# Attention prologue and slots reordered: GpSimd's casts go last, K's spreads and Wo's split are dealt over slots, deviations travel through memory, first V products follow K

## The chip, the cores and the metric

The kernel runs on one core of one Trainium2 chip. The metric is the device time of one execution in microseconds (us). Each kernel is run several times and the median counts; a profiled execution of its own gives the trace.

## What is computed

A decoder layer without masks on 4 x 2048 tokens of width 512: cross attention on a context of 77 keys with 16 heads, then a feed-forward part of inner width 1408 whose activations and weights are rounded to 8 bits.

```python
x = x + xattn(layernorm(x), ctx, ctx, Wq, Wo)
#   Q, K, V = q @ Wq.T, k @ Wq.T, v @ Wq.T          (16 heads of 32)
#   softmax(Q K / sqrt(32)) V, then @ Wo.T
x = x + ffn(layernorm(x), clip_x, clip_down, w_gate, w_up, w_down)
#   xq = round(x / s) * s, one s for the tensor; weights: one s per row
#   h = quant(silu(xq @ Wg) * (xq @ Wu));  h @ Wd
```

## The kernel before, in words

There are three stages, one after the other: `attend` (up to about 650 us of the span), `expand` and `contract`. The change touches `attend` alone.

**Tiles.** The 8192 tokens are 16 blocks of 512. A block is four items (n = 0 to 63 over the whole input). For the projection of queries an item is one group of 128 channels (4 heads) for all 512 tokens of the block; for statistics and the output projection it is one tile of 128 tokens. A batch is 16 items.

**Slots.** `attend` is a software pipeline written out by hand: `for k in SLOTS` from -9 to 72, and every engine runs its own loop over the same k. `at(k, lag)` is item k + lag. TensorE's order in a slot is: scores of item k-2 (`S`, lines 675 and 679), query product of item k+4 (`Q`, line 690, 12 matmuls; the float32 operands are split in a high and a low part, three products each), transposes of the maxima (line 712) when k % 4 is 1 and of the deviations rs (line 703) when it is 3, the products for the maxima of item k+3 (`S`, line 723, called "score matmuls L723" below), output projection of item k-7 (`O`, line 735), sums and values of item k-2 (`DN` line 751, `A` line 754). PSUM banks `A`, `DN`, `O`, `Q` are single, so a transpose into `A` and the values take turns.

**Other engines.** ScalarE makes the high parts (`xT_h`, `qT_h`, `aT_h`), the exponentials and the 8-bit codes of weights (`w_c`, line 509). GpSimd makes the low parts (`aT_l` line 421, `xT_l` line 425, `qT_l` line 429), casts the codes to bf16 (`w_b`, line 413), spreads K over four heads (`kbd`, line 406) and makes Wo's low part (line 432). VectorE does layernorm statistics, maxima (line 593), the scaling of queries by the deviations (`q32`, line 599, which reads `rsb`), the copy of `rsb` out of `A` (line 603), weight maxima and the residual (line 620). SyncE issues every DMA, in order, and waits in between; a wait there holds back all later DMAs.

**Weights.** One of 46 weight steps (22 for gate and up, 24 for down) starts per slot from slot `W_FIRST`: load, one slot later measured and coded, cast in the same slot as coded and at the head of GpSimd's slot, turned by a DMA transpose in slot +2, stored in slot +3.

**Deviations.** After four tiles of statistics rs is a column per tile (128 x 4). The queries need it along the free axis in every partition: TensorE transposes the broadcast columns into `A`, VectorE copies `A` to `rsb`. The wait for that copy sits on TensorE ahead of lines 751 and 754:

```python
if k % 4 == 3 and at(k, 5):
    pe.wait_ge(rsb_rdy, (k + 5) // 4 + 1)
```

A query product of the first item of a block (k % 4 is 0) waits first for all four low parts `xT_l` of its block.

## Time and profile before

| | |
|---|---|
| median of 3 runs | 1185.84 us (1184.47 to 1187.43) |
| profiled execution | 1187.88 us, span 1186.0 us |
| TensorE busy | 1106.8 us of the span |
| VectorE, ScalarE, GpSimd busy | 802.1, 619.7, 401.5 us |
| mean granted TensorE clock | 0.973 of full |

The span is what the trace covers; the time of an execution is some 2 us more. A busy TensorE is one that has matmuls in flight; a gap before a matmul is printed in brackets with the instruction that released it.

### The profile page before, as it was taken

The page shows a single profiled execution, that of the slowest core. Times are in us where ns is not written, and L with a number is a line of the kernel's source. Part 1 is how long each engine was busy: PE and PEld are TensorE (multiplying, and loading weights), DVE is VectorE, ACT ScalarE, POOL GpSimd, SP SyncE. Part 2 cuts the span into 40 slices and gives each one's busy share as a digit, 9 for nine tenths or more (in the row PEclk, how much of TensorE's full clock was granted, in tenths as well). Part 3 has the DMA queues.
Part 4 walks back from the last instruction along what each step waited for, and adds up shares of the span by engine and source line. Part 5 has one row for each costly group of instructions (what it writes and reads, how often), then busy time and mean ns, then how long its engine had stood idle before and what let it go on. Part 6 is the DMA issues. An engine that isn't in the chain of part 4 may idle for free. (4 is left out here: it accounts for less than half of the span.)

```text
span 1186.0 us, 17468 instructions
## 1 busy us (share of the span) xinstructions
PE 1106.8 (93%) x6173; PEld 625.7 (53%) x6202; DVE 802.1 (68%) x1478; ACT 619.7 (52%) x757; POOL 401.5 (34%) x317
## 2 busy tenths in 40 slices
PE   5988999999999999999999969999999999699898
PEld 4645555655666666666665534444444444244333
DVE  5455667677766776766655567787777777566565
ACT  3346555454555555554544436657566664754450
POOL 5454444355353644343321200000000000357578
PEclk8979999999999999999999979999999999799999
DMA  6234556556454545443215626766767512799977
GB/s 238 69 89 110 157 149 160 150 160 152 146 152 143 166 129 164 130 142 104 75 54 161 223 75 230 250 223 234 241 220 253 171 52 89 320 413 418 422 298 261
DMA packets 138736, 219.23 MB, mean 185 GB/s; under 512 B 59040, under 2 KB 67872, under 8 KB 132768
## 3 DMA queue, kind: packets, MB, share of 16 engines
q1 hardware_dynamic: 138656, 218.19, 56.3%
q8 instruction: 46, 0.75, 0.3%
q14 instruction: 34, 0.28, 0.1%
HBM read 133.48 MB, written 72.48 MB: 174 GB/s over the span
## 5 line engine op out<-in xcount | busy, mean ns | idle before, releaser
L1038 POOL TENSOR_TENSOR c_y<-x,c_y 128x512 f32<-128x512 f32 x64 | 112.7, 1794 | 395.2 <-DVE c_y L1072 380.5
L690 PE MATMUL a_Q<-a_xT,wq 128*128 128x512 f32 x768 | 199.8, 410 | 19.0 <-POOL a_xT L425 16.8
L690 PEld LDWEIGHTS a_Q<-a_xT,wq 128*128 128x128 f32 x768 | 144.2, 194 | 73.4 <-issue 22.6
L960 PE MATMUL e_G<-e_cT,gu 128*128 128x512 bf16 x689 | 180.0, 381 | 2.3 <-ACT e_cT L883 1.5
L924 DVE SCALAR_TENSOR_TENSOR h<-e_U,x_gus,e_sg 128x512 f32<-128x512 f32 x176 | 131.8, 749 | 73.2 <-PE e_U L964 47.4
L869 ACT ACTIVATE e_sg<-e_G,x_gus 128x512 f32<-128x512 f32 x176 | 119.0, 685 | 117.6 <-PE e_G L960 117.6
L964 PE MATMUL e_U<-e_cT,gu 128*128 128x512 bf16 x690 | 179.7, 381 | 0.7
L735 PE MATMUL a_O<-a_wo,a_aT 128*128 128x512 f32 x720 | 176.8, 395 | 0.0
L1110 PE MATMUL c_Y<-dn,gu 128*128 128x512 bf16 x704 | 156.8, 386 | 13.5 <-DVE gu L1065 13.5
L501 ACT ACTIVATE a_qT<-a_q 128x512 fp32r<-128x512 f32 x64 | 40.4, 631 | 216.9 <-DVE a_q L599 216.9
L735 PEld LDWEIGHTS a_O<-a_wo,a_aT 128*128 128x128 f32 x720 | 133.4, 189 | 28.0 <-issue 2.5
L472 ACT ACTIVATE a_pr<-a_S 77x2048 f32<-77x2048 f32 x64 | 120.1, 1876 | 37.1 <-PE a_S L679 37.1
L593 DVE TENSOR_REDUCE a_mx<-a_S 128x16 f32<-128x1232 f32 x64 | 92.1, 1439 | 57.4 <-PE a_S L723 57.4
L560 DVE TENSOR_TENSOR a_att<-a_A,a_lnd 128x512 f32<-128x512 f32 x64 | 44.2, 691 | 118.9 <-POOL a_aT L421 61.1
L1110 PEld LDWEIGHTS c_Y<-dn,gu 128*128 128x128 bf16 x704 | 69.4, 99 | 100.6 <-issue 21.0
L421 POOL TENSOR_TENSOR a_aT<-a_att,a_aT 128x512 fp32r<-128x512 f32 x64 | 82.3, 1285 | 113.7 <-ACT a_aT L475 113.7
L1056 ACT ACTIVATE c_c<-h,h_inv 128x3072 int8<-128x3072 f32 (+1 forms) x32 | 82.5, 2633 | 64.9 <-DVE gu L1065 60.4
L960 PEld LDWEIGHTS e_G<-e_cT,gu 128*128 128x128 bf16 x704 | 69.1, 98 | 85.2 <-issue 1.6
L964 PEld LDWEIGHTS e_U<-e_cT,gu 128*128 128x128 bf16 x704 | 69.1, 98 | 83.9 <-issue 1.4
L928 DVE TENSOR_REDUCE e_hm<-h 128x1 f32<-128x512 f32 x160 | 108.0, 675 | 0.0
L429 POOL TENSOR_TENSOR a_qT<-a_q,a_qT 128x512 fp32r<-128x512 f32 x64 | 82.3, 1285 | 62.4 <-ACT a_qT L501 62.4
L413 POOL CAST w_b<-w_c 128x512 bf16<-128x512 int8 (+1 forms) x34 | 20.3, 597 | 195.9 <-ACT w_c L509 195.9
(128 smaller groups left out, 1351.0 us busy)
## 6 DMA issues: line engine op xcount, KB each, us to landing
x<-x_d SPq DMA_DIRECT2D x32, 1024.0 KB, 7.4
h_d<-h SPq DMA_DIRECT2D x24, 1024.0 KB, 4.1
h<-h_d SPq DMA_DIRECT2D x11, 1536.0 KB, 17.2
a_xr<-in_x SPq DMA_DIRECT2D x64, 256.0 KB, 2.9
a_xt<-in_xT SPq DMA_DIRECT2D x64, 256.0 KB, 3.1
x_d<-a_xr SPq DMA_DIRECT2D x64, 256.0 KB, 2.0
a_xs<-in_x SPq DMA_DIRECT2D x60, 256.0 KB, 2.9
out<-c_y SPq DMA_DIRECT2D x15, 1024.0 KB, 9.7
```

The costliest lines, as they stand in the source:

```text
L472: nc.scalar.activation(pr[:], S[0:KEYS], ACT.Exp, scale=SM_SCALE).then_inc(exped, 1)
L593: nc.vector.tensor_reduce(mx5[:, :, :, n.g], S[:, :, 0:HG * KEYS].rearrange("p t (h k) -> p t h k", h=HG), AX.X, ALU.max).then_inc(maxed, 1)
L690: mm = nc.tensor.matmul(Q[:], wq[:, wp, j, P * n.g:P * (n.g + 1)], xT[:, n.par, xp, j], start=(ins == 0), stop=(ins == 3 * KT - 1))
L735: mm = nc.tensor.matmul(projection(n), aT[:, n.par, ap, j, P * n.g:P * (n.g + 1)], wo[:, wp, j], start=(ins == 0), stop=(ins == 3 * KT - 1))
L869: nc.scalar.activation(sg[:, s], G[:, t % GU], ACT.Silu, scale=gus[:, t:t + 1]).then_inc(silued, 1)
L924: nc.vector.scalar_tensor_tensor(out=h[:, place(u, p), t], in0=U[:, t % GU], scalar=gus[:, IT + t:IT + t + 1], in1=sg[:, s], op0=ALU.mult, ...
L928: nc.vector.tensor_reduce(hm[:, p, t - 1:t], h[:, place(u, p), t - 1], AX.X, ALU.max, apply_absolute_value=True)
L960: mm = nc.tensor.matmul(G[:, t % GU], gu[:, t, k], cT[:, p, k], start=(k == 0), stop=(k == KT - 1))
L964: mm = nc.tensor.matmul(U[:, t % GU], gu[:, IT + t, k], cT[:, p, k], start=(k == 0), stop=(k == KT - 1))
L1038: nc.gpsimd.tensor_tensor(y[:, p, t], x1[:, p, t], y[:, p, t], ALU.add).then_inc(added, 1)
L1056: nc.scalar.activation(c8[:, k % 2, lo:hi], h[:, BUFFER[k], lo:hi], ACT.Copy, scale=hinv[:, 0:1]).then_inc(coded, 1)
L1110: mm = nc.tensor.matmul(Y[:, TT * p + t], cb[:, p, j, P * t:P * (t + 1)], dn[:, :, j], start=(j == 0), stop=(j == IT - 1))
```

## The change

In `attend` six things are rearranged. (1) GpSimd's cast of a code goes to the end of its slot, one slot after the coding; turn and store move one slot back as well. `W_FIRST` goes from 1 to 4. (2) The spread of K for the next batch is one quarter per slot in slots 4 to 7 of a batch, not four at once; Wo's high and low parts are made a quarter per slot (ScalarE from slot -1, GpSimd in slots 0 to 3). (3) From block 1 on, rs goes to memory in four column stores at the end of slot 4b-6 and comes back as a broadcast of 128 x 512 one slot later, both in SyncE's queue; only block 0 uses TensorE's transposes. (4) V's products for batches 0 and 1 follow K's at once, then block 0's transposes; V for batches 2 and 3 come in slots -3 and -2. (5) The query product takes its two products with `xT_h` first and waits for `xT_l` before the third; values, not sums, wait for `A`. (6) Some small VectorE and ScalarE work is dropped (`ve`, the copy of `mv1` to `mom`).

```diff
-W_FIRST = 1
+W_FIRST = 4
@@ sync
+                    if (w := weight(k - W_FIRST - 4)) and w.coded:
+                        store_weight(w)
                     if (w := weight(k - W_FIRST - 3)) and w.coded:
-                        store_weight(w)
-                    if (w := weight(k - W_FIRST - 2)) and w.coded:
                         turn_weight(w)
                     if (w := weight(k - W_FIRST)):
                         load_weight(w)
...
+                    if k % 4 == 2 and (n := at(k, 6)) and n.block > 0:
+                        sp.wait_ge(rs_rdy, n.block + 1)
+                        for t in range(TT):
+                            sp.dma_start(rs_d[n.block, t], rs[:, t:t + 1]).then_inc(rs_out, 16)
+                    if k % 4 == 3 and (n := at(k, 5)) and n.block > 0:
+                        sp.wait_ge(rs_out, 16 * TT * n.block)
+                        sp.wait_ge(q_scaled, n.n)
+                        sp.dma_start(rsb[:], rs_d[n.block].rearrange("t p a -> a (t p)").to_broadcast([P, TOK])).then_inc(rsb_in, 16)
@@ gpsimd
                 for k in SLOTS:
-                    if (w := weight(k - W_FIRST - 1)) and w.coded:
-                        pool.wait_ge(w_coded, w.code + 1)
-                        after(pool, w_turned[w.ring], 16 * (w.code // 2), 1 << 30)
-                        nc.gpsimd.tensor_copy(wb[:, w.ring, 0:w.width], wc[:, w.ring, 0:w.width]).then_inc(w_cast, 1)
-                    if k == -5:
-                        pool.wait_ge(mask_in, 16)
-                        pool.wait_ge(k_hi, GROUPS)
-                        spread_k(0)
...
+                    if 0 <= k < KT:
+                        pool.wait_ge(wo_hi, k + 1)
+                        nc.gpsimd.tensor_tensor(wo[:, 1, k], wo32[:, k], wo[:, 0, k].bitcast(F32), ALU.subtract).then_inc(wo_lo, 1)
+                    b, j = k // PER + 1, k % PER - 4
+                    if 0 <= j < HG and 1 <= b < BATCH:
+                        after(pool, m_scored, PER * (b - 1))
+                        spread_k(b, j)
...
+                    if (w := weight(k - W_FIRST - 2)) and w.coded:
+                        pool.wait_ge(w_coded, w.code + 1)
...
@@ vector
                     if (n := at(k, 4)):
                         dve.wait_ge(q_done, n.n + 1)
                         after(dve, qT_l, n.n)
-                        dve.wait_ge(rsb_rdy, n.block + 1)
+                        if n.block > 0:
+                            dve.wait_ge(rsb_in, 16 * n.block)
                         nc.vector.tensor_tensor(q32[:], Q[:], rsb[:], ALU.mult).then_inc(q_scaled, 1)
-                    if k % 4 == 3 and (n := at(k, 5)):
-                        dve.wait_ge(r_turned, n.block + 1)
-                        after(dve, q_scaled, n.n)
-                        nc.vector.tensor_copy(rsb[:], A[:]).then_inc(rsb_rdy, 1)
@@ tensor
+                project_v(0)
+                project_v(1)
+                pe.wait_ge(rs_rdy, 1)
...
+                for t in range(TT):
+                    mm = nc.tensor.transpose(A[:, P * t:P * (t + 1)], rs[:, t:t + 1].to_broadcast([P, P]), id32[:])
...
-                        pe.wait_ge(xT_l, GROUPS * (n.block + 1))
+                        pe.wait_ge(xT_h, GROUPS * (n.block + 1))
...
-                        for wp, xp in ((0, 0), (0, 1), (1, 0)):
+                        for wp, xp in ((0, 0), (1, 0), (0, 1)):
+                            if xp == 1:
+                                pe.wait_ge(xT_l, GROUPS * (n.block + 1))
...
-                    if k % 4 == 3 and (n := at(k, 5)):
-                        pe.wait_ge(rs_rdy, n.block + 1)
...
-                        if k % 4 == 3 and at(k, 5):
-                            pe.wait_ge(rsb_rdy, (k + 5) // 4 + 1)
```

TensorE at the start of the program, from K's products on (`a_S<-p_cx,p_wr`), before:

```order
L643 MATMUL a_S<-p_cx,p_wr 128x308 x48
L703 MATMUL a_A<-id,a_rs 128x128 x4
L690 MATMUL a_Q<-a_xT,wq 128x512 x12
L654 MATMUL a_DN<-p_wr,p_cx 77x512 x12
L690 MATMUL a_Q<-a_xT,wq 128x512 x12
L723 MATMUL a_S<-a_kbd,a_qT 128x308 x4
L654 MATMUL a_O<-p_wr,p_cx 77x512 x12
L690 MATMUL a_Q<-a_xT,wq 128x512 x12
L723 MATMUL a_S<-a_kbd,a_qT 128x308 x4
L654 MATMUL a_DN<-p_wr,p_cx 77x512 x12
```

and of the change:

```order
L659 MATMUL a_S<-p_cx,p_wr 128x308 x48
L670 MATMUL a_DN<-p_wr,p_cx 77x512 x12
L670 MATMUL a_O<-p_wr,p_cx 77x512 x12
L681 MATMUL a_A<-id,a_rs 128x128 x4
L716 MATMUL a_Q<-a_xT,wq 128x512 x24
L739 MATMUL a_S<-a_kbd,a_qT 128x308 x4
L670 MATMUL a_DN<-p_wr,p_cx 77x512 x12
L716 MATMUL a_Q<-a_xT,wq 128x512 x12
L739 MATMUL a_S<-a_kbd,a_qT 128x308 x4
L670 MATMUL a_O<-p_wr,p_cx 77x512 x12
```

V's first two products (into `a_DN` and `a_O`, 12 matmuls each) moved ahead of the transposes of `a_rs` and of all query products.

SyncE in the middle of `attend`, one slot before:

```order
L349 DMA a_xr<-in_x 128x512
L352 DMA x_d<-a_xr 128x512
L355 DMA a_xs<-in_x 128x512
L358 DMA a_xt<-in_xT 128x512
L342 DMA gu_d<-w_T 128x512
L336 DMA_TRANSPOSE w_T<-w_b 128x4x128
L330 DMA w_raw<-in_w_gate 128x512
```

and the slot of the change that begins with the rs stores (they are the end of the slot before it):

```order
L330 DMA w_raw<-in_w_gate 128x512
L378 DMA rs_d<-a_rs 128x1 x4
L349 DMA a_xr<-in_x 128x512
L352 DMA x_d<-a_xr 128x512
L355 DMA a_xs<-in_x 128x512
L358 DMA a_xt<-in_xT 128x512
L342 DMA gu_d<-w_T 128x512
L336 DMA_TRANSPOSE w_T<-w_b 128x4x128
L330 DMA w_raw<-in_w_gate 128x512
L383 DMA a_rsb<-rs_d 128x512
```

Four column stores of `a_rs` and the load of `a_rsb` were added to the queue; between them lie one slot's loads, stores and the DMA transpose.

GpSimd around K's spread for batch 1, before:

```order
L425 TENSOR_TENSOR a_xT<-a_xt,a_xT 128x512
L429 TENSOR_TENSOR a_qT<-a_q,a_qT 128x512
L406 TENSOR_SCALAR a_kbd<-a_kt,a_hmask 128x4x77 x4
L436 CAST id<-id 128x128
L413 CAST w_b<-w_c 128x512
L421 TENSOR_TENSOR a_aT<-a_att,a_aT 128x512
L425 TENSOR_TENSOR a_xT<-a_xt,a_xT 128x512
L429 TENSOR_TENSOR a_qT<-a_q,a_qT 128x512
```

and of the change:

```order
L419 TENSOR_TENSOR a_aT<-a_att,a_aT 128x512
L423 TENSOR_TENSOR a_xT<-a_xt,a_xT 128x512
L427 TENSOR_TENSOR a_qT<-a_q,a_qT 128x512
L412 TENSOR_SCALAR a_kbd<-a_kt,a_hmask 128x4x77
L449 CAST w_b<-w_c 128x512
L419 TENSOR_TENSOR a_aT<-a_att,a_aT 128x512
L423 TENSOR_TENSOR a_xT<-a_xt,a_xT 128x512
L427 TENSOR_TENSOR a_qT<-a_q,a_qT 128x512
```

The spread (`a_kbd`) was a run of four with TensorE's inputs `a_aT`, `a_xT`, `a_qT` behind it, and is now one piece per slot behind them; the cast `w_b` stood ahead of them and now ends the slot.

## Rows read from the trace of the kernel before

**Rows 1.** Timeline, TensorE, steady slots: start us, us, instruction, [idle before <- releaser].

```profile
161.05 1.06 PE L751 MATMUL a_DN<-a_pr,a_ones 77*32 77x512 f32 x8 [0.94 <-DVE a_rsb L603]
...
165.77 3.01 PE L690 MATMUL a_Q<-a_xT,wq 128*128 128x512 f32 x12 [1.71 <-POOL a_xT L425]
168.62 0.73 PE L723 MATMUL a_S<-a_kbd,a_qT 128*128 128x308 f32 x4
...
178.23 0.81 PE L723 MATMUL a_S<-a_kbd,a_qT 128*128 128x308 f32 x4
...
187.50 0.73 PE L723 MATMUL a_S<-a_kbd,a_qT 128*128 128x308 f32 x4
```

**Rows 2.** Timeline, GpSimd, 162 to 166 us, same columns.

```profile
162.63 0.61 POOL L413 CAST w_b<-w_c 128x512 bf16<-128x512 int8 x1 [5.32 <-ACT w_c L509]
...
164.44 1.27 POOL L425 TENSOR_TENSOR a_xT<-a_xt,a_xT 128x512 fp32r<-128x512 f32 x1
```

**Rows 3.** Timeline, TensorE: score matmuls L723 of items 12 and 60.

```profile
137.72 0.82 PE L723 MATMUL a_S<-a_kbd,a_qT 128*128 128x308 f32 x4
...
608.38 0.81 PE L723 MATMUL a_S<-a_kbd,a_qT 128*128 128x308 f32 x4
```

**Rows 4.** Timeline, all engines, the first 38 us.

```profile
9.69 7.32 PE L643 MATMUL a_S<-p_cx,p_wr 128*128 128x308 f32 x48
...
18.97 2.35 DVE L544 TENSOR_TENSOR wq<-p_wc,wq 128x1024 fp32r<-128x1024 f32 x2
...
19.76 5.50 POOL L406 TENSOR_SCALAR a_kbd<-a_kt,a_hmask 128x308 fp32r<-128x308 f32 x4 [1.32 <-ACT a_kt L495]
...
26.54 5.49 PE L690 MATMUL a_Q<-a_xT,wq 128*128 128x512 f32 x12 [6.79 <-POOL a_xT L425]
...
37.61 0.73 PE L723 MATMUL a_S<-a_kbd,a_qT 128*128 128x308 f32 x4
```

**Rows 5.** Timeline, all engines, 56 to 64 us.

```profile
57.07 1.44 DVE L593 TENSOR_REDUCE a_mx<-a_S 128x16 f32<-128x1232 f32 x1 [2.41 <-PE a_S L723]
58.43 0.68 DVE L599 TENSOR_TENSOR a_q<-a_Q,a_rsb 128x512 f32<-128x512 f32 x1
...
59.26 4.57 PE L690 MATMUL a_Q<-a_xT,wq 128*128 128x512 f32 x12 [2.22 <-DVE a_q L599]
...
64.02 0.81 PE L723 MATMUL a_S<-a_kbd,a_qT 128*128 128x308 f32 x4
```

**Rows 6.** Timeline, all engines, 78 to 108 us.

```profile
82.52 1.93 PE L751 MATMUL a_DN<-a_pr,a_ones 77*32 77x512 f32 x8 [3.12 <-DVE a_rsb L603]
...
99.87 0.82 PE L723 MATMUL a_S<-a_kbd,a_qT 128*128 128x308 f32 x4
...
107.54 0.83 PE L723 MATMUL a_S<-a_kbd,a_qT 128*128 128x308 f32 x4 [0.47 <-ACT a_pr L472]
```

**Rows 7.** Windows: busy us (instructions) by engine, PEclk, DMA share, GB/s.

```profile
80.00:85.00 5.00, 2.48 (x12) 0.68 (x16) 3.07 (x6) 1.84 (x3) 3.99 (x6) 0.52 0.37 113
...
230.00:240.00 10.00, 10.00 (x68) 6.65 (x67) 7.52 (x21) 5.36 (x8) 4.35 (x4) 1.00 0.65 155
```

**Rows 8.** Timeline of SyncE's queue around the only 4-byte column stores, L368.

```profile
547.05 1.85 SPq L368 DMA_DIRECT2D dsc_d<-w_dsc  x4
550.33 0.33 SPq L349 DMA_DIRECT2D a_xr<-in_x  x1
```

**Rows 9.** Landing in us: the first of those stores; then the last two, min/median/max.

```profile
dsc_d<-w_dsc SPq DMA_DIRECT2D x1, 0.5 KB, 4.0
...
DMA to landing us min/median/max: 6.9/7.8/8.7
```

**Rows 10.** DMA issues of 549 to 556 us, and of the whole run: KB each, us to landing.

```profile
a_xr<-in_x SPq DMA_DIRECT2D x1, 256.0 KB, 9.3
...
a_xs<-in_x SPq DMA_DIRECT2D x1, 256.0 KB, 6.6
...
dscale<-dsc_d SPq DMA_DIRECT2D x1, 256.0 KB, 3.5
```

More of the change, by code:

```diff
@@ L364, in _ @@
                         load_weight(w)
-                    if k == W_FIRST + WSTEPS + 4:
+                    if k == W_FIRST + WSTEPS + 5:
                         sp.wait_ge(w_scaled, 2 * IT + KT)
@@ L429, in _ @@
                         nc.gpsimd.tensor_tensor(qT[:, n.ring, 1], q32[:], qT[:, n.ring, 0].bitcast(F32), ALU.subtract).then_inc(qT_l, 1)
-                    if k == -1:
-                        pool.wait_ge(w_split, 1)
-                        nc.gpsimd.tensor_tensor(wo[:, 1], wo32[:], wo[:, 0].bitcast(F32), ALU.subtract).then_inc(w_split, 1)
-                    if k == 2:
-                        spread_k(1)
-                        pool.wait_ge(id_in, 16)
+                    if k == -5:
+                        nc.gpsimd.memset(mx[:], 0.0).then_inc(mx_zero, 1)
+                        nc.gpsimd.memset(ones[:], 1.0).then_inc(consts, 1)
+                        pool.wait_ge(c_in, 16)
+                        nc.gpsimd.tensor_copy(negw[:], neg[:].unsqueeze(2).to_broadcast([P, GROUPS, KEYS])).then_inc(consts, 1)
+                        pool.wait_ge(mask_in, 16)
+                        pool.wait_ge(k_hi, GROUPS)
+                        for j in range(HG):
+                            spread_k(0, j)
+                    if 0 <= k < KT:
[5 more added lines that the diff above has]
+                        spread_k(b, j)
+                    if k == 8:
                         nc.gpsimd.tensor_copy(id16[:], id32[:])
-                    b = k // PER + 1
-                    if k % PER == 3 and 2 <= b < BATCH:
-                        pool.wait_ge(m_scored, PER * (b - 1))
-                        spread_k(b)
+                    if (w := weight(k - W_FIRST - 2)) and w.coded:
+                        pool.wait_ge(w_coded, w.code + 1)
+                        after(pool, w_turned[w.ring], 16 * (w.code // 2), 1 << 30)
+                        nc.gpsimd.tensor_copy(wb[:, w.ring, 0:w.width], wc[:, w.ring, 0:w.width]).then_inc(w_cast, 1)
             @block.scalar
@@ L479, in _ @@
                         nc.scalar.activation(xT[:, n.par, 0, n.g], xt32[:, n.n % RINGX], ACT.Copy).then_inc(xT_h, 1)
-                    if k == -7:
+                    if k % 4 == 2 and (n := at(k, 9)) and n.block > 0:
+                        root(n.block)
+                    if k == -5:
                         for n in range(2):
@@ L580, in _ @@
                         own.step(nc.vector.bn_stats(bst1[:], t))
-                        nc.vector.tensor_reduce(mv1[:, n.g, 3:4], t, AX.X, ALU.min)
-                        own.step(nc.vector.bn_aggr(mv1[:, n.g, 0:2], bst1[:]))
-                        nc.vector.tensor_copy(mom[:, n.block, n.g], mv1[:, n.g]).then_inc(mom_rdy, 1)
+                        nc.vector.tensor_reduce(mom[:, n.block, n.g, 3:4], t, AX.X, ALU.min)
+                        nc.vector.bn_aggr(mom[:, n.block, n.g, 0:2], bst1[:]).then_inc(mom_rdy, 1)
                     if k % 4 == 1 and (n := at(k, -1)):
@@ L693, in _ @@
                         mm.then_inc(q_done, 1)
-                    if k % 4 == 3 and (n := at(k, 5)):
-                        pe.wait_ge(rs_rdy, n.block + 1)
-                        after(pe, att_rdy, k - 2)
-                        if n.block == 0:
-                            pe.wait_ge(centred, KT)
-                            pe.wait_ge(id_in, 16)
-                        after(pe, rsb_rdy, n.block)
-                        for t in range(TT):
-                            mm = nc.tensor.transpose(A[:, P * t:P * (t + 1)], rs[:, t:t + 1].to_broadcast([P, P]), id32[:])
-                        mm.then_inc(r_turned, 1)
                     if k % 4 == 1 and (n := at(k, -1)):
@@ L726, in _ @@
                     if (n := at(k, -7)):
-                        pe.wait_ge(w_split, 2)
+                        after(pe, wo_lo, KT)
                         after(pe, aT_l, n.n - n.g + 4)
@@ L738, in _ @@
                         mm.then_inc(projected, 1)
-                    if 0 <= k + 4 < BATCH:
-                        project_v(k + 4)
+                    if 2 <= k + 5 < BATCH:
+                        project_v(k + 5)
                     if now:
                         pe.wait_ge(exped, now.n + 1)
-                        after(pe, att_rdy, now.n)
-                        if k % 4 == 1 and at(k, -1):
-                            pe.wait_ge(mT_rdy, k // 4 + 1)
-                        if k % 4 == 3 and at(k, 5):
-                            pe.wait_ge(rsb_rdy, (k + 5) // 4 + 1)
                         after(pe, ln_done, now.n)
@@ L752, in _ @@
                         mm.then_inc(summed, 1)
+                        after(pe, att_rdy, now.n)
+                        if k % 4 == 1 and at(k, -1):
+                            pe.wait_ge(mT_rdy, k // 4 + 1)
                         for h in range(HG):
```

82 lines of the change are left out of this document (45 added, 37 removed).

## The prediction, on record before the run

> **What bounds the kernel now.** I read the waits of `attend` first, then TensorE's timeline, then what released each gap. The span is 1186.0 us (table above) and `attend` takes the first 650. In steady slots TensorE is the bound: score matmuls L723 follow each other at 178.23 - 168.62 = 9.61 us in a slot with transposes of the maxima and at 187.50 - 178.23 = 9.27 us without [rows 1], and no gap lies between. Once per block it stands still twice: 0.94 us for the copy of `rsb` (after its own transposes), then 1.71 us for `xT_l` [rows 1]. Between items 12 and 60 the 48 slots, 12 blocks, take 608.38 - 137.72 = 470.66 us, 39.22 a block [rows 3], against 9.61 + 3 x 9.27 = 37.42 us of a block without gaps.
>
> Why is `xT_l` late? GpSimd's cast waited 5.32 us for a code that ScalarE makes at the end of the same slot, and only behind it come `aT_l` and `xT_l`, which ends at 165.71; the query product starts at 165.77 [rows 2, 1]. So the slack of an idle engine is thrown away by its order.
>
> The prologue has one large gap: K's products end at 17.0, then GpSimd spreads K from 19.76 to 25.3 ahead of the last `xT_l`, and the first query product starts at 26.54 after a gap of 6.79 us and runs 5.49 us, where one at full clock is done in 165.77 to 168.62, 2.85 us [rows 4, 1]. A second weak place is near 82 us: TensorE waits 3.12 us for `rsb` (VectorE copies late), the granted clock falls to 0.52 of full, near the level of 1.2 GHz [rows 6, 7].
>
> **The change, part by part.**
>
> *Steady blocks (items 12 to 60).* The cast behind the low parts removes the 1.71 us; no `rsb` copy on TensorE's path removes the 0.94; the transposes of rs, 0.3 us, go. ScalarE still keeps up: it does so in the gapless slots now, with the same work. So 12 blocks x (39.22 - 37.42) = 21.6 us. The spread of K in quarters is some 1.4 us of GpSimd behind the low parts in slots that leave it 5 us idle [rows 2]; it costs nothing there, and would cost its 1.4 only where GpSimd ends after the next query product needs it.
>
> *Prologue.* V0 and V1 fill the gap: K's products end at 17.0; with 2.9 us for each (12 matmuls, as the query product) V1 ends at 22.9, transposes 23.3. The inputs that VectorE makes must be there by then: before, it finished Wq's low part, its last, at 18.97 + 2.35 = 21.3 [rows 4]; centring and statistics only swap places ahead of it, so I keep that time, with 2 us to spare. Query product 0 runs at full clock 23.3 to 26.2, item 1 follows after VectorE's scaling (0.7 and a hop) at 27.1, and L723 of item 0 comes at 30.0, not 37.61 [rows 4]. Gain there 7.6 us. The two remaining V go in the next two slots, 6.5 us each (2.9 for V, 2.9 for the query product, 0.7 for L723), so L723 of items 1, 2 come at 36.5 and 43.0. Slot 0 has no V left and is bound by VectorE: maxima 1.44 and scaling 0.68 [rows 5] must pass between L723 and the next query product. So query product 4 starts at 45.8, and L723 of item 3 at 48.7. Its scaled query could be done at 51.4.
>
> *The way through memory.* This is the unknown price. The trace has the same two forms once each. Four column stores of 128 x 1 start at 547.05; the last is issued at 548.5 and lands 8.7 us later, 557.2, 10.1 after the first issue [rows 8, 9]. Transfers behind them are held too: a load issued at 550.33 took 9.3, one of the next slot 6.6 us [rows 8, 10]. The broadcast load took 3.5 in a free queue [rows 10]; behind such stores I take up to the 6.6. SyncE needs some 0.3 us to go on, so rs is back in `rsb` 10.4 + 3.5 = 13.9 to 10.4 + 6.6 = 17.0 us after the first store; between ends that are both seen I take the middle, 15.4. The Trainium skill (DMA: Bandwidth & Descriptors, Specifications and Latency) says that below 512 B a transfer is a read-modify-write and that the fixed cost of a DMA is about 2 us; by that, two in turn are 4 us and the stores would be hidden everywhere. No row here shows a column store as short.
>
> In steady slots the first store follows the scaling of slot 4b-6 by 1 us; `rsb` is needed 18.6 us after that scaling, and TensorE misses the scaled query only some 3 us later (its L735, L751, L754 and scores lie between). 16.4 fits, 18.0 too. Queued behind SyncE's wait for the stores are residual, `xs` and weight transfers; `xs` is issued some 3.4 us after the scaling and needed at about 13.6 (my estimate from VectorE's order), and at 6.6 to 9.3 us to landing is there by 10.0 to 12.7.
>
> In the prologue slots are 6.4 us and it does not fit. *Block 1:* slot -2 ends its scaling at 39.3 (L723 of item 1, maxima, scaling), rs follows at 40.2 and the first store with it; `rsb` is back at 55.6 (54.1 to 57.2), where VectorE wants it at 50.8. SyncE's queue and VectorE stand behind it. Query product 5 then starts at 56.3 at the lower clock, as it does now after a gap (4.57 us [rows 5]), and L723 of item 4 comes at 61.2 (59.8 to 62.8), not 64.02. Gain so far 2.8 us (1.2 to 4.2): over half of the 7.6 is given back.
>
> *Items 4 to 12.* Before, 137.72 - 64.02 = 73.7 us [rows 5, 3]. Now: slots 2 to 4 take TensorE's own 6.4 each (9.27 less the 2.85 of an output projection, of as many matmuls as a query product), with neither the wait of 3.12 nor the low clock. Slot 5, with transposes of the maxima and a wait for `A`, 7.0. There block 2's `rsb` is late: stores from 71.2, `rsb` back at 86.6 (85.1 to 88.2); TensorE could go on at 83.8 and does, a scaling later, at 87.5: a stall of 3.7 (2.2 to 5.3), and some 2 us (0 to 4) of lower clock behind it. Slot 6 has no output projection yet, and weights have begun: ScalarE's chain sets 7.6, as it does now: 107.54 - 99.87 = 7.67, with L723 released by the exponential [rows 6]; slot 7 the same, slots 8 and 9 are 9.3 and 9.6. Sum 19.2 + 7.0 + 3.7 + 2 + 15.2 + 18.9 = 66.0, gain 7.7 (4.1 to 11.2). `W_FIRST` at 4 keeps weight work out of slots 2 to 4; the last weight step is coded in slot 50, stored by 53, long before slot 60 needs it.
>
> *Rest.* The last items, `expand` and `contract` keep their order: 0. The dropped VectorE pieces (`ve`, the copy of moments) lie on an engine that waits for TensorE: 0; if VectorE were the bound, they would be 0.2 us a slot.
>
> Sum: 2.8 + 7.7 + 21.6 = 32.1 us. Against the profiled execution's 1187.88 that is 1155.8, against its span 1153.9; that execution is 2.0 above the median, so the median goes from 1185.84 to 1153.7.
>
> **Rivals.**
>
> *Memory route hidden (0.2).* If all four stores land in 4.0 us, as their first did [rows 9] (I don't know why the later ones took longer), `rsb` is at hand in time. Then L723 of item 4 comes at 51.4 + 4.6 + 0.4 = 56.4, gain 7.6; items 4 to 12 gain 13.5; with 21.6 the sum is 42.7: 1143.2. Against: 8.7 and 9.3 us in [rows 9, 10]. The figures of the Trainium skill's DMA page would lead here.
>
> *The stores hold the queue in every block (0.17).* In steady slots with weights the DMA share is 0.65 [rows 7]: 24 us of work in a block of 37.4, and 10 us in which the queue trickles leave 3. If `xs`, the DMA transpose or `rsb` come late by more than VectorE's slack, each of the 12 blocks loses 1 to 1.7 us again: 12 to 20 us, 1165 to 1173, about 1168.
>
> *Slower than before (0.03).* The same mechanism at a larger price: `rsb` would have to come later than 18.6 + 3.4 + 2.7 = 24.7 us after the scaling, since 32.1 / 12 = 2.7 us of stall a block cancels all. At 4 us a block it is 1186 + 16 = 1202. Nothing landed that late.
>
> *The order doesn't help (0.05).* `xT_l` stays late because ScalarE's `xT_h`, not the cast, sets it. Then 12 x 1.1 us stay, 1167. Against: GpSimd waits for the code alone, with ScalarE's `aT_h` long done.
>
> **How the numbers follow.** Likeliest 0.55: 1153.7, its own range 1146 to 1162 from the bounds above. With the hidden route (1143) and most of the held queue (1168) the range is 1141 to 1168. A measurement of this kernel tells about 0.3%, 3.5 us. Faster 0.96, same 0.01, slower 0.03.
>
> **What would show it.** Right: no gap of TensorE released by `xT_l` or `rsb` in items 12 to 60, L723 there at 37.4 us a block; L723 of item 0 at 30; in block 1 a gap of 4 to 8 us ahead of query product 5 whose releaser is VectorE's scaling, and there a wait for the DMA `rsb`; a lower clock behind it. The stores landing in 4 to 9 us each. Wrong: stores landing in 2 to 4 us and no such gap (1143), or VectorE waiting for `xs` or `rsb` in each block (1168).

## The result, and the profile after

The changed kernel takes 1153.82 us, median of four runs (1151.84 to 1156.43), against 1186.55 before (four runs; the 1185.84 of the prediction is the median of three): a ratio of 0.9724, with a 95% interval of 0.9711 to 0.9737. The forecast was 1153.7. The profiled execution is the one of 1156.43; it stands to the profiled one of before, 1187.88, at 31.5 us less (forecast 32.1).

The page of the changed kernel, its span, TensorE's busy time, the granted clock by slices, and the DMA packets:

```profile
span 1154.6 us, 17335 instructions
...
PE 1096.4 (95%) x6142; PEld 616.8 (53%) x6142; DVE 764.8 (66%) x1383; ACT 619.8 (54%) x760; POOL 403.0 (35%) x321
...
PEclk9899999999999999999999989999999999899999
...
DMA packets 149535, 223.18 MB, mean 193 GB/s; under 512 B 67920, under 2 KB 76752, under 8 KB 143568
```

TensorE's busy time fell by 10 us only (1106.8 before); the other 21 us that were won had been idle time. The windows of the changed kernel say where idle time is left (busy us by engine, granted clock, DMA share):

```profile
40.00:62.00 22.00, 13.05 (x51) 10.41 (x50) 6.46 (x11) 4.34 (x8) 8.75 (x7) 0.77 0.44 106
62.00:94.00 32.00, 27.68 (x183) 16.67 (x182) 14.72 (x25) 18.00 (x25) 18.14 (x15) 0.89 0.38 85
120.00:560.00 440.00, 440.00 (x2879) 285.37 (x2877) 301.13 (x658) 247.21 (x338) 206.81 (x183) 1.00 0.62 162
```

In the 440 us from 120 on TensorE is busy without a break at full clock. What `attend` still loses lies mostly ahead of 110 us and at item 60. Before, the stretch had gaps, but not the two of [rows 1] in each block: of the twelve blocks between items 12 and 60, four have a gap of 1.7 us for `xT_l`, two one of 0.5 us and six none; the gap for `rsb` is 0.9 us in four blocks and 0.4 us in eight. Timeline of the kernel before, TensorE, two later blocks:

```profile
327.56 3.01 PE L690 MATMUL a_Q<-a_xT,wq 128*128 128x512 f32 x12 [0.47 <-POOL a_xT L425]
...
362.78 1.06 PE L751 MATMUL a_DN<-a_pr,a_ones 77*32 77x512 f32 x8 [0.39 <-DVE a_rsb L603]
...
365.72 3.02 PE L690 MATMUL a_Q<-a_xT,wq 128*128 128x512 f32 x12
```

The score matmuls (line L739 now, L723 before) split the gain. Item 12 moved from 137.72 to 128.45, item 60 from 608.38 [rows 3] to 577.23:

```profile
128.45 0.82 PE L739 MATMUL a_S<-a_kbd,a_qT 128*128 128x308 f32 x4
...
577.23 0.84 PE L739 MATMUL a_S<-a_kbd,a_qT 128*128 128x308 f32 x4
```

| stretch | before, us | after, us | gain | forecast |
|---|---|---|---|---|
| start to item 4 | 64.02 | 61.60 | 2.4 | 2.8 |
| items 4 to 12 | 73.70 | 66.85 | 6.9 | 7.7 |
| items 12 to 60 | 470.66 | 448.78 | 21.9 | 21.6 |

Below, "the slot of item n" is the stretch from the score matmuls of item n-1 to those of item n. The loss in the first 62 us is next. Items 0 to 3 come at 30.26, 36.37, 42.42 and 48.21 (forecast 30.0, 36.5, 43.0, 48.7), so up to item 3 some 7 to 8 us are won. Then block 1's deviations are late. Timeline of the changed kernel, SyncE's issues (SPq), VectorE and TensorE:

```profile
39.87 1.76 SPq L378 DMA_DIRECT2D rs_d<-a_rs  x4
...
41.67 0.43 SPq L355 DMA_DIRECT2D a_xs<-in_x  x1
...
48.21 0.72 PE L739 MATMUL a_S<-a_kbd,a_qT 128*128 128x308 f32 x4
49.41 0.33 SPq L383 DMA_DIRECT2D a_rsb<-rs_d  x1
49.78 0.43 SPq L355 DMA_DIRECT2D a_xs<-in_x  x1
52.33 0.69 DVE L590 BATCH_NORM_STATS2 a_bst<-a_xs 128x6 f32<-128x512 f32 x1 [7.10 <-DMA a_xs<-in_x]
...
54.81 0.69 DVE L615 TENSOR_TENSOR a_q<-a_Q,a_rsb 128x512 f32<-128x512 f32 x1 [0.25 <-DMA a_rsb<-rs_d]
...
55.65 5.46 PE L716 MATMUL a_Q<-a_xT,wq 128*128 128x512 f32 x12 [6.72 <-DVE a_q L615]
```

SyncE issues the four column stores at 39.87 and can load `rsb` only at 49.41, when they have landed; that load takes 5.3 us and is there at 54.7. The load of `xs` that VectorE waits 7.10 us for is not the one of 49.78, behind SyncE's wait (nothing waits for that one). It is the one of 41.67, issued ahead of the wait and directly behind the stores. It took 10.6 us to land, at 52.27:

```profile
a_xs<-in_x SPq DMA_DIRECT2D x1, 256.0 KB, 10.6
```

So the stores delay two transfers: `rsb`, which has to wait for them, and `xs`, which is queued behind them. VectorE takes 2.2 us for the statistics of `xs` and the maxima, and then waits 0.25 us for `rsb`. With `xs` in time it would have waited for `rsb` until the same 54.7; the larger wait bears the name of the transfer that comes first. TensorE stands still for 6.72 us, and its next query product takes 5.46 us at the lower clock. The slot of item 8 (slot 5) repeats it, with block 2:

```profile
71.44 1.75 SPq L378 DMA_DIRECT2D rs_d<-a_rs  x4
...
73.23 0.43 SPq L355 DMA_DIRECT2D a_xs<-in_x  x1
...
81.83 0.33 SPq L383 DMA_DIRECT2D a_rsb<-rs_d  x1
...
84.30 0.69 DVE L590 BATCH_NORM_STATS2 a_bst<-a_xs 128x6 f32<-128x512 f32 x1 [3.90 <-DMA a_xs<-in_x]
...
86.60 1.57 PE L699 MATMUL a_S<-a_qT,a_kt 32*77 32x512 f32 x12 [2.41 <-DVE a_mx L608]
...
87.19 0.69 DVE L615 TENSOR_TENSOR a_q<-a_Q,a_rsb 128x512 f32<-128x512 f32 x1 [0.64 <-DMA a_rsb<-rs_d]
...
88.53 4.77 PE L716 MATMUL a_Q<-a_xT,wq 128*128 128x512 f32 x12
```

Here TensorE stops first for the maxima, which stand behind the statistics of `xs` in VectorE's order, and not for the query. The `xs` is again the one behind the stores, issued at 73.23 and 11.0 us on its way. Over `attend` the waits of the changed kernel (us in total, times, longest) name both transfers, though TensorE waits four times only:

```profile
DVE a_bst L590 <- DMA a_xs<-in_x: 35.3, 15, 7.1
...
PE a_Q L716 <- DVE a_q L615: 11.0, 4, 6.7
...
DVE a_q L615 <- DMA a_rsb<-rs_d: 9.4, 6, 4.6
```

One of VectorE's 15 waits for `xs` is of the program's start (0.7 us); the other 14 stand in blocks 1 to 14, each for the `xs` issued behind the stores, which takes 10.5 to 11.9 us there. (Block 15 has no `xs` to load any more.) From block 3 on the waits are 0.9 to 2.9 us, and from 120 us on no gap of TensorE follows them.

### The profile page after: what moved, and what is told of

It is laid out like the page before. It is cut to its first block and busy times, and to the rows that moved or that the text cites. A ratio compares the mean times of both kernels' runs of the same rounds, so it can differ in the third digit from the quotient of the medians.

```text
span 1154.6 us, 17335 instructions
## 1 busy us (share of the span) xinstructions
PE 1096.4 (95%) x6142; PEld 616.8 (53%) x6142; DVE 764.8 (66%) x1383; ACT 619.8 (54%) x760; POOL 403.0 (35%) x321
## 5 line engine op out<-in xcount | busy, mean ns | idle before, releaser
L716 PE MATMUL a_Q<-a_xT,wq 128*128 128x512 f32 x768 | 197.1, 407 | 11.0 <-DVE a_q L615 11.0
L423 POOL TENSOR_TENSOR a_xT<-a_xt,a_xT 128x512 fp32r<-128x512 f32 x64 | 82.5, 1291 | 1.9 <-ACT a_xT L496 1.9
```

Of the source, the lines that this page charges most:

```text
L716: mm = nc.tensor.matmul(Q[:], wq[:, wp, j, P * n.g:P * (n.g + 1)], xT[:, n.par, xp, j], start=(ins == 0), stop=(ins == 3 * KT - 1))
```

## The experiments

Every ratio is to the kernel before, with its 95% interval; the changed kernel stands at 0.9724 [0.9711, 0.9737]. MEM_FROM is the first block that uses the way through memory; blocks below it keep TensorE's transposes and VectorE's copy.

**All blocks by transposes.**

```diff
+MEM_FROM = 16
-                    if k % 4 == 2 and (n := at(k, 6)) and n.block > 0:
+                    if k % 4 == 2 and (n := at(k, 6)) and n.block >= MEM_FROM:
...
+                    if k % 4 == 3 and (n := at(k, 5)) and 0 < n.block < MEM_FROM:
...
+                            mm = nc.tensor.transpose(A[:, P * t:P * (t + 1)], rs[:, t:t + 1].to_broadcast([P, P]), id32[:])
...
+                        if k % 4 == 3 and (n := at(k, 5)) and 0 < n.block < MEM_FROM:
+                            pe.wait_ge(rsb_rdy, n.block + 1)
```

> The change, but the deviations of every block go through TensorE's transposes and VectorE's copy, none through memory. Theory A (the route through memory costs the prologue, and TensorE's order absorbs a copy): L739-type score matmuls of item 4 come near 55.5 us instead of 61.6 (6 us), slot 5 loses its stall and low clock (4.7 us), item 60 its late rsb (1.6 us), and 0.3 us of transposes come back in each of 12 steady blocks (3.6 to 5 us): 1153.8 - 12.3 + 4 = 1145.5 us. Theory B (the memory route pays in steady blocks, as a wait of 0.4 to 0.9 us for the copy comes back beside the 0.3): 1153.8 - 12.3 + 12 x 1.1 = 1155 us.

Measured: 1151.02 us, 0.9703 [0.9683, 0.9723]. A steady block takes 37.70 us instead of 37.27 (its length where nothing stalls), 0.43 more, so the way through memory earns 12 x 0.43 = 5.2 us in steady blocks. In the prologue it costs: from item 0 to item 8 this kernel takes 56.5 us and the changed one 63.2. That is the upper end, though: six of the kernels below leave this stretch of the changed kernel as it is or nearly so (cast first, old product order, both, `dsc` later, one store, weights from slot 8), and they take 59.3 to 62.3. So the price is 3 to 7 us, different from execution to execution, and the sum of both is near nothing: the intervals of the two kernels overlap. The other edits, not this one, carry most of the steady gain: 39.22 - 37.70 = 1.52 of the 1.8 us a block.

**Transposes in blocks 1 and 2 only** (the same edit with MEM_FROM = 3).

> The change, but blocks 1 and 2 take TensorE's transposes and only blocks 3 to 15 go through memory. Theory A: the 6 + 4.7 us of the prologue come back, steady blocks stay at 37.3 us, item 60 keeps its stall: 1153.8 - 10.7 + 0.6 = 1143.7 us. Rival: the stalls near 50 and 86 us are set by VectorE and a low clock whatever way rs takes; then 1153 us.

Measured: 1148.89 us, 0.9672 [0.9656, 0.9688]. This is faster than the changed kernel by 4.9 us, clear of both intervals: the memory route does cost in the prologue. Item 8 comes at 85.72, item 12 at 120.80, and then come the blocks of the changed kernel. It is 5.2 us short of what was expected, and the trace says where: the slots of items 3 and 4 take 7.4 and 7.7 us (in both the query product runs at the lower clock, 4.57 us, behind a gap of 2.22), and in the slot of item 7 the values wait 2.0 us for VectorE's copy of `rsb`, which must follow the scaling that still reads the old one.

**The cast back at the head of the slot**, in the slot of the coding; a code's turn and store come one slot earlier with it.

```diff
+                    if (w := weight(k - W_FIRST - 1)) and w.coded:
+                        pool.wait_ge(w_coded, w.code + 1)
+                        after(pool, w_turned[w.ring], 16 * (w.code // 2), 1 << 30)
+                        nc.gpsimd.tensor_copy(wb[:, w.ring, 0:w.width], wc[:, w.ring, 0:w.width]).then_inc(w_cast, 1)
                     if (n := at(k, -3)):
...
-                    if (w := weight(k - W_FIRST - 2)) and w.coded:
```

> The change, but GpSimd casts at the head of its slot, in the slot of the coding (turn and store one slot earlier too). Theory A (as the prediction priced it: the cast's place is worth the 1.71 us gap of each block with weights, some 9 blocks): 1153.8 + 15 = 1169 us, with gaps of TensorE released by xT_l. Theory C (the query product that takes the high parts first hides a low part that is 1.7 us late, since its third product starts 1.9 us after its first): 1153.8 to 1155.5 us, no such gap.

**The query product's old order (low part of x second), the cast last.**

```diff
-                        pe.wait_ge(xT_h, GROUPS * (n.block + 1))
+                        pe.wait_ge(xT_l, GROUPS * (n.block + 1))
...
-                        for wp, xp in ((0, 0), (1, 0), (0, 1)):
-                            if xp == 1:
-                                pe.wait_ge(xT_l, GROUPS * (n.block + 1))
+                        for wp, xp in ((0, 0), (0, 1), (1, 0)):
```

> The change, but a query product waits for all low parts before its first matmul, as before the change; GpSimd's cast stays last. Either of the two edits is enough (theory C): GpSimd has the last xT_l done some 5 us ahead, so nothing waits: 1153.8 us, no gap. If the cast's place alone is not enough (rival), 0.5 to 1.7 us of gap in the blocks with weights: 1158 to 1165 us.

**Both undone.**

> The change with both undone: cast at the head of GpSimd's slot, and a query product that waits for all low parts before its first matmul. Theories A and C both expect the gap of 1.7 us back in the blocks with weights in each slot and some 0.5 us in the others: 1153.8 + 10 to 15 = 1164 to 1169 us. If it stays at 1154, neither edit was what removed the gap, but the spread of K or the dropped copies.

Measured: 1151.91 us, 0.9708 [0.9691, 0.9726], with the cast at the head; 1152.85, 0.9716 [0.9700, 0.9732], with the old product order; 1162.14, 0.9784 [0.9768, 0.9801], with both undone. One row pair of the third, TensorE's and GpSimd's timeline, shows the gap that the change was to remove:

```profile
190.71 1.26 POOL L427 TENSOR_TENSOR a_xT<-a_xt,a_xT 128x512 fp32r<-128x512 f32 x1
...
192.02 3.02 PE L714 MATMUL a_Q<-a_xT,wq 128*128 128x512 f32 x12 [1.48 <-POOL a_xT L427]
```

And the first, cast at the head:

```profile
185.68 0.61 POOL L419 CAST w_b<-w_c 128x512 bf16<-128x512 int8 x1 [4.29 <-ACT w_c L525]
...
186.62 3.42 PE L716 MATMUL a_Q<-a_xT,wq 128*128 128x512 f32 x12
...
187.49 1.30 POOL L427 TENSOR_TENSOR a_xT<-a_xt,a_xT 128x512 fp32r<-128x512 f32 x1
...
188.84 0.76 PEld L716 LDWEIGHTS a_Q<-a_xT,wq 128*128 128x128 f32 x4 [0.56 <-POOL a_xT L427]
```

There the cast waited 4.29 us for its code and the low part is late, as before: it is ready at 188.79. But the query product has begun at 186.62 with the eight matmuls that don't read it, and only the last four wait, in this block for some 0.4 us, in the block ahead of it not at all. From item 12 to item 63 the kernel with both undone takes 483.81 us. The changed one takes 475.70, or 474.1 without its stall at item 60, which this kernel doesn't have: 9.7 us are lost, and 8.3 between the medians. In seven of its blocks, one of them ahead of item 12, a slot takes 10.2 to 12.3 us instead of 9.2. With the cast alone put back the stretch takes 474.60 us, with the old product order alone 474.07. Either edit alone removes nearly all of the loss; the second adds nothing that the medians show.

**Is it the number of stores, or what they hold?** One store of all 512 values, and eight column stores (the same four to a second place).

```diff
-                        for t in range(TT):
-                            sp.dma_start(rs_d[n.block, t], rs[:, t:t + 1]).then_inc(rs_out, 16)
+                        sp.dma_start(rs_d[n.block].rearrange("t p a -> p (t a)"), rs[:], allow_slow_non_contiguous=True).then_inc(rs_out, 16)
```

> The change, but rs goes to memory in one store of 512 elements of 4 bytes a block and not in four stores of 128. Theory per element (the stores are slow because of their 512 elements of 4 bytes): rsb stays late in blocks 1 and 2 and the queue behind it too: 1153.8 us within 2. Theory per store (each store costs its own 2 us or so in the queue): the column is out 5 us earlier, the stall of 6.7 us in block 1 falls to about 1.5, block 2 has none: 1153.8 - 9 = 1145 us.

> The change, with each column stored twice (the second to a spare place), so eight column stores a block, and SyncE waits for all eight. The rival of the held queue says what a longer hold would do: rsb some 8 us later in every block, 24 us after the scaling where 18.6 + 3.4 are free: a stall of 1 to 2 us in each of 12 steady blocks and 8 us more in each of blocks 1 and 2: 1153.8 + 34 = 1188 us. If the hold doesn't grow with the stores (they overlap), 1154 to 1160 us.

Measured: 1153.00 us, 0.9723 [0.9703, 0.9743], with one store: no difference. The store is issued at 39.05 and the load of `rsb` at 48.62, 9.57 us later, against 49.41 - 39.87 = 9.54 with four. With eight: 1266.23 us, 1.0676 [1.0628, 1.0724], slower than the kernel before. Its timeline in a steady block:

```profile
299.91 1.75 SPq L378 DMA_DIRECT2D rs_d<-a_rs  x4
...
301.70 1.86 SPq L380 DMA_DIRECT2D rs_d<-a_rs  x4
...
304.56 0.43 SPq L355 DMA_DIRECT2D a_xs<-in_x  x1
...
319.89 0.33 SPq L385 DMA_DIRECT2D a_rsb<-rs_d  x1
...
320.93 0.69 DVE L592 BATCH_NORM_STATS2 a_bst<-a_xs 128x6 f32<-128x512 f32 x1 [8.77 <-DMA a_xs<-in_x]
```

The load of `rsb` follows 19.98 us after the first store, twice the time for twice the values, so the price goes by the values of 4 bytes (some 19 ns each) and not by the instructions. And the `xs` issued behind the eight stores, 4.65 us after the first, takes 16.3 us to land: in each of blocks 1 to 14 VectorE waits 7.3 to 13.5 us for such a load, 134.3 us over the run (35.3 above). That is the rival "the stores hold the queue in every block", made real by a factor of two. My expectation was far too small: it counted `rsb` alone, with 1 to 2 us a block, where `xs` is the larger wait, and the traces show one or two slots of 10.6 to 18.0 us in each block, the lower clock behind the gaps included.

**V1 in its slot.** On the kernel with MEM_FROM = 3; V1 no longer precedes the first transposes, V1 to V3 come in slots -3 to -1.

```diff
                 project_v(0)
-                project_v(1)
...
-                    if 2 <= k + 5 < BATCH:
-                        project_v(k + 5)
+                    if 1 <= k + 4 < BATCH:
+                        project_v(k + 4)
```

> Transposes for blocks 1 and 2 as in the kernel with that label, and V's product of batch 1 not ahead of the query products but in slot -3, batches 2 and 3 one slot later each. Only one V product fills the first gap (Wq's low part comes at 20.7 us), so score matmuls of item 0 come 2.9 us earlier, at 26.3; slot -1 gets a V product that covers the 2.2 us wait for VectorE and keeps the clock up, so the query product after it takes 2.9 and not 4.57 us. Score matmuls of item 3 at 49.1 - 2.9 - 1.3 = 44.9, total 1148.9 - 4.2 = 1144.7 us. Rival: the query products wait for their low parts instead of the V product; then item 0 stays at 29 and the total is 1147.5 us.

Measured: 1146.06 us, 0.9656 [0.9636, 0.9675]. Item 0 comes at 28.23, not at the 26.3 expected. 1.1 us of this is the start of this execution: V0 begins at 17.66, and at 16.59 in the profile of the kernel with MEM_FROM = 3 alone. From V0's start item 0 takes 10.6 us and there 12.6, so one V product ahead of the query products instead of two saves 2.0 of its 2.9 us. Item 6 at 67.92 is 2.2 us ahead of that kernel (70.10). But the slot of item 7 took 11.8 us instead of 8.8 there, and behind it nothing of the lead is left in this profile (item 12 at 121.63 and 120.80). The profile is the slowest of the four executions, 1148.06; two others took 1144.8. Rows of the slot of item 7, TensorE, and then those of the kernel without this edit:

```profile
71.77 1.93 PE L783 MATMUL a_A<-a_pr,a_v 77*32 77x512 f32 x8 [2.02 <-DVE a_rsb L621]
...
75.55 4.35 PE L721 MATMUL a_Q<-a_xT,wq 128*128 128x512 f32 x12
```

```profile
73.95 1.06 PE L785 MATMUL a_A<-a_pr,a_v 77*32 77x512 f32 x8 [2.02 <-DVE a_rsb L622]
...
76.03 3.04 PE L723 MATMUL a_Q<-a_xT,wq 128*128 128x512 f32 x12
```

The gap is the same 2.02 us, with the same releaser. Behind it one kernel runs at the lower clock for most of 8 us (0.60 of full in the mean of 72 to 80 us) and the other at full clock.

**Block 2's transposes in bank O.** On the last kernel. Bank `O` is idle until the output projection begins, so the values need not wait for the copy out of `A`; the first output projections wait for the copy out of `O` instead.

```diff
+                        nc.vector.tensor_copy(rsb[:], (O if n.block == 2 else A)[:]).then_inc(rsb_rdy, 1)
...
+                        R = O if n.block == 2 else A
                         for t in range(TT):
-                            mm = nc.tensor.transpose(A[:, P * t:P * (t + 1)], rs[:, t:t + 1].to_broadcast([P, P]), id32[:])
+                            mm = nc.tensor.transpose(R[:, P * t:P * (t + 1)], rs[:, t:t + 1].to_broadcast([P, P]), id32[:])
...
+                        if n.n < 4:
+                            pe.wait_ge(rsb_rdy, 3)
```

> Theory A: in the kernel with V1 in slot -3 and TensorE's transposes for blocks 1 and 2 (measured 1146.1), slot 7 took 11.8 us because the values of item 3 waited 2.0 us for VectorE's copy of rsb out of bank A, and because the clock then fell (values 1.9 instead of 1.1, query product 4.4 instead of 3.0, together some 3 us). With block 2's transposes in bank O, which nothing else uses yet, the wait and the low clock go: item 7 at 75 instead of 79.7, median 1141 to 1142. Theory B: only the wait of 2.0 goes, the clock falls whatever is done there: 1144. Theory C: TensorE waits for the same copy or for VectorE's maxima elsewhere: 1146.

Measured: a ratio of 0.9625 [0.9612, 0.9637], the fastest version of all. The median is 1143.3 us over six runs; one of them took 3396.41 us and stands in no ratio, the other five lie between 1140.83 and 1144.60, with a median of 1142.71. Timeline, TensorE:

```profile
67.20 0.60 PE L732 MATMUL a_O<-id,a_rs 128*128 128x128 f32 x4
...
71.41 3.04 PE L721 MATMUL a_Q<-a_xT,wq 128*128 128x512 f32 x12
...
74.31 0.83 PE L753 MATMUL a_S<-a_kbd,a_qT 128*128 128x308 f32 x4
```

No gap, full clock, and the slot of item 7 takes 6.6 us instead of 11.8: 5.2 us for the 2.0 that were waited. Between the medians it is 3.4 us. That fits the first theory, that the lower clock goes with its gap, but one profile of each kernel can't show it: with the same gap and full clock, as in the kernel with MEM_FROM = 3 alone, the slot took 8.8 us.

**The load of `rsb` behind the load of `xs`.** On the changed kernel.

```diff
-                    if k % 4 == 3 and (n := at(k, 5)) and n.block > 0:
...
+                    if k % 4 == 0 and (n := at(k, 4)) and n.block > 0:
                         sp.wait_ge(rs_out, 16 * TT * n.block)
```

> The changed kernel with the load of rsb issued one slot later in SyncE's order, behind the load of xs, so that no xs load waits for the column stores. Theory A (what costs in block 1 and 2 is rsb itself; xs behind SyncE's wait was late by 7.1 and 3.9 us but rsb landed only 0.2 and 0.6 us after VectorE had worked xs off): VectorE's waits for xs shrink and the same time goes into the wait for rsb, items 4 and 8 move by under 1.5 us, median 1152.5 to 1154. Theory B (xs is the stall): items 4 and 8 come 2 to 3 us sooner each, median 1149. Theory C (in steady blocks rsb, issued later, comes late): 1156 or more, with VectorE's waits for rsb in every block.

Measured: 1161.95 us, 0.9790 [0.9771, 0.9808], slower than the changed kernel. The edit doesn't do what my expectation says of it: the `xs` that VectorE waits for was ahead of SyncE's wait already, and still stands behind the stores (issued at 41.07 here, 10.0 us to landing, waited for 6.5 us). What the edit brings forward is the next `xs`, to 42.02, and nothing waited for that one. In block 1 VectorE then waits 2.39 us for `rsb`, issued at 48.69 and 6.9 us on its way, so item 4 comes at 61.46 (61.60 before this edit): a longer wait for `rsb` takes the place of a shorter one for `xs`. In steady blocks `rsb` is now too late, as its timeline shows:

```profile
192.22 0.40 SPq L360 DMA_DIRECT2D a_rsb<-rs_d  x1
...
197.02 0.69 DVE L615 TENSOR_TENSOR a_q<-a_Q,a_rsb 128x512 f32<-128x512 f32 x1 [2.83 <-DMA a_rsb<-rs_d]
```

VectorE waits 33.1 us for it over all blocks, and the slots of items 20, 24, 40 and 52 take 0.5 to 1.1 us more each. The profiled run (1159.89) has item 63 only 2.0 us later than the changed kernel's; the rest of the 8 us between the medians can't be placed.

**Weights from slot 8.** On the changed kernel, `W_FIRST = 8`.

> The changed kernel with the weight steps from slot 8 instead of 4. Theory A (my step: in slots 6 and 7 ScalarE's chain, with weights begun, sets 7.6 us): the slots of items 8 to 10 come down from 7.7 and 8.4 us by 0.5 to 1 each; the dsc stores also leave block 15's rs stores, and the slot of item 60 takes 9.6 instead of 11.2: median 1150.5 to 1151.5. Theory B (ScalarE's attention work alone sets these slots): only the 1.6 us at item 60, 1152.2. Theory C: the later end of the weights costs at the end of attend: 1155.

Measured: 1148.14 us, 0.9671 [0.9658, 0.9684]. The two slots after item 8 take 6.61 us each instead of 7.69 and 8.43, TensorE's own time, 2.9 us together, and the slot of item 60 takes 9.56 instead of 11.16. The direction is that of the first theory, the sizes are larger. In this profile the slot of item 8 itself takes 9.04 instead of 11.98: TensorE's gap is 1.31 us and not 2.41, and the clock stays full behind it. That is not to be put down to the weights: with weights from slot 4 the kernel with one store took 9.19 us there and the one with both edits undone 9.74.

**The stores of `dsc` one slot later.** On the changed kernel. They follow block 15's four stores directly, `rsb` lands 12 us after its issue, and the slot of item 60 takes 11.16 us. Timeline of the changed kernel there:

```diff
-                    if k == W_FIRST + WSTEPS + 5:
+                    if k == W_FIRST + WSTEPS + 6:
```

```profile
551.14 1.75 SPq L378 DMA_DIRECT2D rs_d<-a_rs  x4
553.88 1.95 SPq L368 DMA_DIRECT2D dsc_d<-w_dsc  x4
...
560.77 0.32 SPq L383 DMA_DIRECT2D a_rsb<-rs_d  x1
...
572.85 0.69 DVE L615 TENSOR_TENSOR a_q<-a_Q,a_rsb 128x512 f32<-128x512 f32 x1 [4.58 <-DMA a_rsb<-rs_d]
```

> The changed kernel with the four column stores of dsc one slot later, so that they follow rsb's load and not the rs stores. Theory A (eight column stores in a row held rsb back at item 60: issued 8.3 us after the first store, landed 12 us later): the slot of item 60 takes 9.6 instead of 11.2 us, VectorE's 4.6 us wait for rsb goes, median 1152.2. Theory B (the stall at item 60 has another cause, say the loads of the end): the slot stays at 11.2, 1153.8.

Measured: 1151.84 us, 0.9702 [0.9689, 0.9714]; the slot takes 9.56 us and VectorE's wait there is gone. The interval overlaps narrowly with the changed kernel's. And the kernel with the old product order, whose SyncE queue is that of the changed kernel, also had 9.55 us in this slot, with a wait of 1.44 us only: the stall comes in some executions and not in others, so its share of the median is under 1.6 us.

## Why the prediction was right, and which of its reasons were not

The sum met the median to 0.1 us, and that closeness is luck: four executions of the changed kernel spread over 4.6 us, and the three stretches were off by -0.4, -0.8 and +0.3 us, the last with a stall of 1.6 us in it that the sum didn't have.

*Steady blocks.* The size was right (21.6 forecast, 21.9 measured, in which a stall of 1.6 us at item 60 is contained; without it a block takes 37.27 us instead of my 37.42). It was right because it is a difference of two measured lengths, 39.22 and a block without gaps; how the gaps make it up was read wrongly. I took both gaps of [rows 1] for those of each block, and they are those of one block in three (above); 0.94 and 1.71 sum to more than the 1.8 us a block that were to be explained. The reason was half right as well. I wrote that the cast behind the low parts removes the gap for `xT_l`. The runs show that the new order of the query product's three parts does so too: with the cast back at the head 0.5 us are lost in all, with both undone 9.7 us. I should have asked how long the product can run on what it has: eight of twelve matmuls take some 2 us, more than the 1.71 of the gap.

The steady blocks won 21.9 + 1.6 = 23.5 us. If the parts add up, the runs account for 14.9 of it: 9.7 us for the cast and the product's order together, 5.2 us for the way through memory. The other 8.6 us belong to edits that no run undoes. The likely one is the wait for the copy, which in the changed kernel stands behind the sums and not ahead of them: with transposes and copies in all blocks no gap of 0.2 us or more is left between items 12 and 60, where the kernel before had 6.7 us of gaps for `rsb`. That is argued, not shown.

*Prologue.* Right in each of items 0 to 3 within 0.6 us, with K's products starting 0.8 us later in this profile than in that of before (10.51 and 9.69). That V0 and V1 fill the gap was the wrong reason: they take its time, and what removes it is GpSimd's order: the last low part of block 0 stood behind K's spread, whose end was 25.3 [rows 4], and now all four are done at 16.88, ahead of it. With V1 in its slot the first query product starts at 20.93 without a wait, and item 0 comes 2.0 us sooner after V0's start.

*The way through memory.* The size was right: `rsb` could be used 54.81 - 39.87 = 14.9 us after the first store (forecast 15.4, 13.9 to 17.0), item 4 at 61.60 (61.2), the gap 6.72 us with the lower clock behind it. What it does to its neighbours was only half seen. I named `xs` as queued behind SyncE's wait for the stores; the one that matters is issued ahead of that wait and stands behind the stores themselves. I gave it 6.6 to 9.3 us to landing and found room for it in steady slots; it took 10.5 to 11.9, so that VectorE waits in each of these blocks. And I left it out of the prologue, where it costs VectorE 7.10 us in block 1 and sets TensorE's gap in block 2. In block 1 the stall would have been as long without it, since `rsb` lands at 54.7 either way. Not run: the loads of `xs` issued ahead of the stores. The Trainium skill (DMA: Bandwidth & Descriptors, Latency and other measured facts) has about 2 us of fixed cost for a transfer. The measurements differ from it here: 512 values of 4 bytes hold the queue for 9.5 us, in one store or in four, and 1024 for 20.0. The rival "memory route hidden", which those figures would give, was wrong.

*Items 4 to 12.* 66.85 us for the 66.0 forecast: the slots of items 5 to 7 take 6.34, 6.96 and 6.60 (6.4 each forecast), the stall and its clock 11.98 (7.0 + 3.7 + 2), and slots 6 and 7 of my sum, 7.69 and 8.43 (7.6 each). TensorE's gaps in these two, 0.97 and 1.71 us, end with ScalarE's exponential. That weights are what makes the chain that long is borne out by the run with weights from slot 8, where both slots fall to 6.61. The stall's size was partly luck: in profiles whose code up to there is the same or nearly so its slot took 9.0 to 12.0 us.

*Edits costed at nothing.* K's spread and Wo's split dealt over slots, the dropped VectorE pieces: no run takes them apart. The 440 us without a gap show only that they cost nothing there, not what they gave.

*The rivals.* "The stores hold the queue in every block" was closer than its price of 1168 made it look: its sign, VectorE waiting for `xs` in each block, is there in blocks 1 to 14, and twice the values give 1266 us. What decides is that its slack is just enough in steady slots. "Slower than before" was this mechanism with a larger price, and the same run shows it. "The order doesn't help" fell: no wait of TensorE for `xT` is left in the changed kernel.

What stays open: why equal gaps are followed by full clock in one profile and by half in another, and what a version with bank O and weights from slot 8 together would take; it was not run.

## What to carry to other kernels

A store of one column of 4-byte values costs by its values, and every transfer queued behind it pays too, whether it depends on the store or not. Count those transfers as well as the value you send, and in the short slots of a prologue above all, where the same route that is free in steady state can cost as much as it earns: use two routes, one for the prologue and one for the rest. When a wait names a load, look up when that load was issued and how long it took; the next load of the same tile is easily taken for it. When two edits aim at one gap, undo each alone and both together: here either was enough, and only the pair of undoings showed the gap. Read a gap in every block before you call it the gap of each block. A gap's price is the wait and, in some executions, the lower clock behind it: a slot with 2.0 us of waiting was 2.2 us longer at full clock and 5.2 us at the lower.

## What the runs showed of the hardware

Four stores of 128 x 4 bytes and one store of 512 x 4 bytes take equally long from the first issue to the load that waits for them, 9.54 and 9.57 us in block 1; eight take 19.98 in a steady block. Loads issued behind them are held: 10.5 to 11.9 us to landing for an `xs` load of 256 KB behind four, 12.1 to 18.0 behind eight, where the median was 2.9 us in the kernel before. Over the run that median rose to 4.8 us, and that of `rsb` is 6.8 us although its issue comes after the stores have landed:

```profile
a_xs<-in_x SPq DMA_DIRECT2D x60, 256.0 KB, 4.8
...
a_rsb<-rs_d SPq DMA_DIRECT2D x15, 256.0 KB, 6.8
```

The length of a gap doesn't tell the clock behind it. Behind the 2.02 us of the slot of item 7 the clock was once full and once half, in kernels that differ in where V1 stands. Behind the gap in the slot of item 8 it was full after 1.31, 1.88, 2.23 and 2.61 us (weights from slot 8, one store, both edits undone, old product order) and lower after 1.61, 2.06 and 2.41 (cast first, `dsc` later, changed kernel). And behind 2.22 us ahead of the query product of item 4, the changed kernel and the one with MEM_FROM = 3:

```profile
45.37 3.00 PE L716 MATMUL a_Q<-a_xT,wq 128*128 128x512 f32 x12 [2.22 <-DVE a_q L615]
...
44.73 4.57 PE L723 MATMUL a_Q<-a_xT,wq 128*128 128x512 f32 x12 [2.22 <-DVE a_q L618]
```

The Trainium skill (TensorE: Matmul & The Clock Gate, What's actually happening) says that the number of matmuls at the low clock at a kernel's start varies from run to run of one kernel. The rows above show the like behind gaps in the middle of one, and no row says which it will be.
